# Quantised feed-forward: single-precision rows turned by TensorE, input rows weighted by GpSimd in two passes

## The reference

```
def activation_quant(x):
    scale = 127.0 / max(max(abs(x), axis=-1), 1e-5)
    return clip(round(x * scale), -128, 127) / scale
def weight_quant(w):
    scale = 1.0 / max(mean(abs(w)), 1e-5)
    return clip(round(w * scale), -1, 1) / scale
def bitlinear(x, w, g):
    return einsum('bsd,od->bso', activation_quant(rmsnorm(x, g)), weight_quant(w))

x = layernorm(h)                       # mean and variance over the 192
u, v = bitlinear(x, w_in, g_in)        # 2 x 512 columns, split in two
y = u * silu(v)
h + bitlinear(y, w_out, g_out)         # back to 192 columns
```

## Time and profile before

| | us |
|---|---|
| median of 3 runs | 2757.29 |
| lowest and highest run | 2749.5, 2757.34 |
| profiled execution, span from first to last instruction | 2748.1 |
| profiled execution, time around its span | not given in the page |
| stretch of the 28 chunks, first transpose to last `ho` | 2322.7 to 2744.9 |
| mean granted TensorE clock over the span | 0.895 |

### The profile page before, as it was taken

How to read it: one execution, slowest core, us unless ns; L and a number is a source line. 1 busy time by engine, 2 the same in 40 slices (tenths; PEclk the granted TensorE clock), 3 DMA queues, 4 the chain that set the end, 5 groups by cost and what they waited for, 6 DMA issues and landing times. The chain is left out here.

```text
span 2748.1 us, 45420 instructions
## 1 busy us (share of the span) xinstructions
PE 2290.8 (83%) x14046; PEld 1660.5 (60%) x14047; DVE 1996.1 (73%) x5437; ACT 1551.7 (56%) x2693; POOL 1004.0 (37%) x1024
## 2 busy tenths in 40 slices
PE   8999999999996999999937999926778794666665
PEld 4444444444444888888827999925576684444443
DVE  5777777777763899999944444447698877899986
ACT  2444444444444788888734565536566551777776
POOL 1100100100000266566652444478787720344433
PEclk9999999999998999999958999957688886777776
DMA  2000000000002011111136777721111100000000
GB/s 57 0 18 13 0 18 13 0 9 1 0 0 90 16 53 51 51 52 52 51 111 221 257 252 258 238 77 50 46 48 43 46 9 22 21 26 21 26 26 26
DMA packets 69143, 162.81 MB, mean 59 GB/s; under 512 B 12977, under 2 KB 32342, under 8 KB 68702
## 3 DMA queue, kind: packets, MB, share of 16 engines
q1 hardware_dynamic: 39426, 94.27, 10.4%
q0 software_dynamic: 21504, 44.99, 5.8%
q10 hardware_dynamic: 8064, 21.68, 2.6%
HBM read 63.98 MB, written 63.88 MB: 47 GB/s over the span
## 5 line engine op out<-in xcount | busy, mean ns | idle before, releaser
L211 ACT ACTIVATE prob<-pscore 128x896 f32<-128x896 f32 x336 | 308.0, 917 | 423.9 <-PE pscore L293 423.9
L418 DVE TENSOR_REDUCE pmax<-ppre 112x1 f32<-112x512 f32 x656 | 424.5, 686 | 162.0 <-PE ppre L260 161.9
L307 PE MATMUL pout<-prob,xkey 128*64 128x448 f32 x1344 | 328.3, 567 | 0.4 <-ACT prob L211 0.4
L260 PE MATMUL ppre<-xh,yh 49*112 49x512 f32 x656 | 291.4, 446 | 7.8 <-DVE pmax L418 4.2
L723 POOL DMA_INDIRECT rows_in<-xr,idx x224 | 241.3, 1077 | 127.1 <-DVE idx L1249 69.5
L193 POOL CAST yh<-ynext 113x448 fp32r<-113x448 f32 x28 | 17.2, 614 | 667.5 <-DVE pmax L418 639.4
L260 PEld LDWEIGHTS ppre<-xh,yh 49*112 49x112 f32 x656 | 112.7, 172 | 239.8 <-issue 103.5
L1708 POOL DMA_INDIRECT yg<-rows_out,place x224 | 229.3, 1024 | 62.4 <-issue 62.1
L293 PE MATMUL pscore<-yh,xh 49*128 49x448 f32 x700 | 241.1, 422 | 0.4 <-DVE yh L438 0.4
L2223 POOL TENSOR_TENSOR yg<-y,gout 112x512 f32<-112x512 f32 x112 | 141.1, 1270 | 258.6 <-DVE y L2456 258.6
L1558 POOL TENSOR_TENSOR zl<-z,zh 128x448 fp32r<-128x448 f32 x126 | 144.5, 1147 | 218.3 <-ACT zh L1524 208.8
(11 more groups left out here) (388 smaller groups left out, 6558.0 us busy)
## 6 DMA issues: line engine op xcount, KB each, us to landing
wd<-down SPq DMA_DIRECT2D x63, 512.0 KB, 3.0
xb<-rows_in SPq DMA_DIRECT2D x63, 448.0 KB, 3.6
rows_out<-yb ACTq DMA_DIRECT2D x63, 336.0 KB, 3.1
out<-ho SPq DMA_DIRECT2D x28, 336.0 KB, 2.8
rows_in<-zero SPq DMA_DIRECT2D x15, 448.0 KB
rows_in<-xr,idx POOLq DMA_INDIRECT x224
yg<-rows_out,place POOLq DMA_INDIRECT x224
xkey<-in_xkey SPq DMA_DIRECT2D x4, 800.0 KB, 6.6
```

The source lines that it names most:

```text
L211: nc.scalar.activation(prob[j % 3][:, :, :], pscore[j % 2][:, :, 0:CH], ACT.Exp).then_inc(exped, 1)
L260: pe.matmul(out[:, :], yh1[rows, q * T:(q + 1) * T], xh[b % 2][rows, block * 512:(block + 1) * 512], start=True, stop=True, tile_position= ...
L307: mm = pe.matmul(pout[i * LO:(i + 1) * LO, 0:CH], xkey[b % 2][:, 2 * j + i, :], prob[j % 3][:, i, :], start=(j == 0), stop=(i == 1 and j = ...
L418: nc.vector.reduce_max(pmax[:, q, 2 * block + half:2 * block + half + 1], bank(u, depth), AX.X).then_inc(pre_max, 1)
```

## The change

Four things change together.

- `xq` and `yq`, the bf16 copies of the rounded rows, are gone, and with them VectorE's subtraction and ScalarE's `whole_y`. TensorE turns `xr` and `yr` themselves, in single precision, with the f32 identity `eye`. MAGIC is subtracted where ScalarE copies the turned rows out of PSUM (`bias=-MAGIC`, to bf16).
- `pxt` and `pyt` give way to one PSUM tile `ptr` of three banks. A group of four transposes fills 448 columns of one bank; the groups go round the three banks, numbered by `first_x` and `first_y`, and each is copied out by itself: four copies for y and two for x, in place of two and one.
- `weigh_in` moves from VectorE to GpSimd and becomes two instructions for the whole chunk, `xd` = `h` - mean and `xg` = `xd` x `gin`. It runs three chunks ahead, behind `root_of(g)`.
- `xg` has two buffers.

```diff
+            def weigh_in(g):
+                if g:
+                    pool.wait_ge(S["xg_out"], g)
+                nc.gpsimd.tensor_tensor(xd[:], h[:, g * TPC:(g + 1) * TPC, :],
+                                        mean[:, g * TPC:(g + 1) * TPC].unsqueeze(2).broadcast_to([T, TPC, D]),
+                                        ALU.subtract).then_inc(S["xd_out"], 1)
+                pool.wait_ge(S["xd_out"], g + 1)
+                if g >= 2:
+                    pool.wait_ge(S["xr_out"], g - 1)
+                nc.gpsimd.tensor_tensor(xg[g % 2][:], xd[:], gin[:].unsqueeze(1).broadcast_to([T, TPC, D]),
+                                        ALU.mult).then_inc(S["xg_out"], 1)
+
+            pool.wait_ge(S["gin_in"], 16)
+            weigh_in(0)
+            weigh_in(1)
...
             for g in range(NC):
+                if g == 0:
+                    weigh_in(2)
                 weigh(g, 0)
                 weigh(g, 1)
                 root_of(g)
+                if g + 3 < NC:
+                    weigh_in(g + 3)
...
             def transpose_y(g):
-                pe.wait_ge(S["yq_out"], 2 * g + 2)
-                for half in range(2):
-                    for k in range(2):
-                        for q in range(TPC):
-                            mm = pe.transpose(pyt[:, half, k * CH + q * T:k * CH + (q + 1) * T],
-                                              yq[:, q, (2 * half + k) * 128:(2 * half + k + 1) * 128], eyeb[0:T, 0:T])
-                    mm.then_inc(S["ytr_mm"], 1)
+                pe.wait_ge(S["ya_out"], g + 1)
+                pe.wait_ge(S["yr_out"], g + 1)
+                for k in range(4):
+                    n = first_y[g] + k
+                    if n >= 3:
+                        pe.wait_ge(S["tr_out"], n - 2)
+                    for q in range(TPC):
+                        mm = pe.transpose(ptr[:, n % 3, q * T:(q + 1) * T], yr[:, q, k * 128:(k + 1) * 128],
+                                          eye[0:T, 0:T])
+                    mm.then_inc(S["tr_mm"], 1)
...
-            def whole_y(g, pair):
-
-                act.wait_ge(S[("ya_out", "yr_out")[pair]], g + 1)
-                nc.scalar.activation(yq[:, 2 * pair:2 * pair + 2, :], yr[:, 2 * pair:2 * pair + 2, :],
-                                     ACT.Copy, bias=-MAGIC).then_inc(S["yq_out"], 1)
-
             def take_y(g):
-                for half in range(2):
-                    act.wait_ge(S["ytr_mm"], 2 * g + half + 1)
-                    nc.scalar.copy(yT[:, 2 * half:2 * half + 2, :],
-                                   pyt[:, half, 0:2 * CH].rearrange("p (k c) -> p k c", k=2)).then_inc(S["yT_out"], 1)
+                for k in range(4):
+                    n = first_y[g] + k
+                    act.wait_ge(S["tr_mm"], n + 1)
+                    nc.scalar.activation(yT[:, k, :], ptr[:, n % 3, 0:CH], ACT.Copy, bias=-MAGIC).then_inc(
+                        S["tr_out"], 1)
...
-            def weigh_in(g):
-
-                for q in range(TPC):
-                    t = g * TPC + q
-                    ins_ = nc.vector.scalar_tensor_tensor(xg[:, q, :], h[:, t, :], mean[:, t:t + 1], gin[:],
-                                                          ALU.subtract, ALU.mult)
-                ins_.then_inc(S["xg_out"], 1)
...
                 for q in range(TPC):
-                    ins_ = nc.vector.tensor_scalar(xr[:, q, :], xg[:, q, :], sx[:, q:q + 1], MAGIC, ALU.mult, ALU.add)
+                    ins_ = nc.vector.tensor_scalar(xr[:, q, :], xg[g % 2][:, q, :], sx[:, q:q + 1], MAGIC, ALU.mult, ALU.add)
                 ins_.then_inc(S["xr_out"], 1)
-                dve.wait_ge(S["xr_out"], g + 1)
-                if g:
-                    dve.wait_ge(S["xtr_mm"], g)
-                nc.vector.tensor_scalar(xq[:], xr[:], MAGIC, None, ALU.subtract).then_inc(S["xq_out"], 1)
```

More of the change, by code:

```diff
@@ L2161, in bit_ffn_phase @@
         tmp2 = sb("tmp2_5", [T, NT])
-        xg = sb("xg5", [T, TPC, D])
+        xd = sb("xd5", [T, TPC, D])
+        xg = [sb(f"xg5_{i}", [T, TPC, D]) for i in range(2)]
         xr = sb("xr5", [T, TPC, D])
-        xq = sb("xq5", [T, TPC, D], BF16)
         xT = sb("xT5", [KC, 2, CH], BF16)
@@ L2194, in bit_ffn_phase @@
         out_t = out.rearrange("b (t p) d -> p (b t) d", p=T)
+        first_x, first_y, turned = [0], [], 2
+        for g in range(NC):
+            if g:
+                first_y.append(turned)
+                turned += 4
+            if g + 1 < NC:
+                first_x.append(turned)
+                turned += 2
+        first_y.append(turned)
         @block.sync
@@ L2244, in transpose_in @@
             def transpose_in(g):
-                if g:
-                    pe.wait_ge(S["xT_out"], g)
-                pe.wait_ge(S["xq_out"], g + 1)
-                for q in range(TPC):
-                    for c in range(2):
-                        mm = pe.transpose(pxt[:, c, q * T:(q + 1) * T], xq[:, q, c * KC:(c + 1) * KC], eyeb[0:T, 0:T])
-                mm.then_inc(S["xtr_mm"], 1)
+                pe.wait_ge(S["xr_out"], g + 1)
+                for c in range(2):
+                    n = first_x[g] + c
+                    if n >= 3:
+                        pe.wait_ge(S["tr_out"], n - 2)
+                    for q in range(TPC):
+                        mm = pe.transpose(ptr[0:KC, n % 3, q * T:(q + 1) * T], xr[:, q, c * KC:(c + 1) * KC],
+                                          eye[0:T, 0:T])
+                    mm.then_inc(S["tr_mm"], 1)
             def into(g, q):
@@ L2263, in transpose_y @@
             def transpose_y(g):
-                pe.wait_ge(S["yq_out"], 2 * g + 2)
-                for half in range(2):
-                    for k in range(2):
-                        for q in range(TPC):
-                            mm = pe.transpose(pyt[:, half, k * CH + q * T:k * CH + (q + 1) * T],
-                                              yq[:, q, (2 * half + k) * 128:(2 * half + k + 1) * 128], eyeb[0:T, 0:T])
-                    mm.then_inc(S["ytr_mm"], 1)
+                pe.wait_ge(S["ya_out"], g + 1)
+                pe.wait_ge(S["yr_out"], g + 1)
+                for k in range(4):
+                    n = first_y[g] + k
+                    if n >= 3:
+                        pe.wait_ge(S["tr_out"], n - 2)
+                    for q in range(TPC):
+                        mm = pe.transpose(ptr[:, n % 3, q * T:(q + 1) * T], yr[:, q, k * 128:(k + 1) * 128],
+                                          eye[0:T, 0:T])
+                    mm.then_inc(S["tr_mm"], 1)
             def enter(g):
-                pe.wait_ge(S["xT_out"], g + 1)
+                pe.wait_ge(S["tr_out"], first_x[g] + 2)
                 into(g, 0)
@@ L2315, in take_x @@
             def take_x(g):
-                act.wait_ge(S["xtr_mm"], g + 1)
-                nc.scalar.copy(xT[:, :, :], pxt[:, :, :]).then_inc(S["xT_out"], 1)
+                for c in range(2):
+                    n = first_x[g] + c
+                    act.wait_ge(S["tr_mm"], n + 1)
+                    nc.scalar.activation(xT[:, c, :], ptr[0:KC, n % 3, 0:CH], ACT.Copy, bias=-MAGIC).then_inc(
+                        S["tr_out"], 1)
             def silu(g, q):
@@ L2378, in _ @@
         def _(dve):
-            def weigh_in(g):
-                for q in range(TPC):
-                    t = g * TPC + q
-                    ins_ = nc.vector.scalar_tensor_tensor(xg[:, q, :], h[:, t, :], mean[:, t:t + 1], gin[:],
-                                                          ALU.subtract, ALU.mult)
-                ins_.then_inc(S["xg_out"], 1)
             def largest_in(g):
                 dve.wait_ge(S["xg_out"], g + 1)
-                nc.vector.tensor_reduce(am[:], xg[:], AX.X, ALU.max, apply_absolute_value=True).then_inc(S["am_out"], 1)
+                nc.vector.tensor_reduce(am[:], xg[g % 2][:], AX.X, ALU.max, apply_absolute_value=True).then_inc(S["am_out"], 1)
             step = [0]
```

33 lines of the change are left out of this document (13 added, 20 removed).

## The result

| | before | after |
|---|---|---|
| median of the runs, us | 2753.39 (4 runs, 2749.41 to 2757.34) | 2797.32 (4 runs, 2796.96 to 2797.73) |
| ratio after to before, 95% interval | 1 | 1.0156 [1.014, 1.0171] |
| span of the profiled execution, us | 2748.1 | 2795.9 |
| mean granted TensorE clock over the span | 0.895 | 0.892 |
| mean period of the first 24 chunks, us | 14.61 | 16.79 |

The kernel became 44 us slower. The forecast was slower by 71 us, with 2768 to 2860 us as its range. Direction and mechanism hold, the size was too large. Ratios leave out two slow runs: one of e3 (4511.79 us) and one of the kernel before beside e5 to e8 (3732.81 us, granted clock 0.547).

What follows compares the result with a forecast made beforehand. The bound was taken as a chain of waits through ScalarE, TensorE and VectorE, period 14.52 us. 25 x (2.66 + 0.19) = 71 us on the 2748.1 us span, with 9.2 around it, gave 2828 us, range 2768 to 2860.

Steps and rivals of the forecast that it cites:

- The collision: Behind root `r`, VectorE's small steps stand still until GpSimd's running pass ends, delaying `yr` by 2.66 us a chunk.
- A: Rival for the small steps: no collision that matters, VectorE works as if alone; 2732 us, faster; chance 12%.
- B: Rival for the small steps: only pass one stands in the way, +1.1 us a chunk; 2789 us; chance 13%.
- D: Rival for GpSimd's passes: each takes 2.54 us, stall +4.1 us a chunk; 2864 us; chance 10%.
- C: Rival for TensorE: collision, but its clock stays high, tile 2's products lose 0.8 us; 2808 us; chance 10%.
- The stall of +2.66 us: Small steps behind `r`: `yr` starts at P + 4.51 against P + 1.85, in each of 25 chunks.
- `s2` to the third `y`, +0.19 us: TensorE's stretch: dropping `yq` saves 1.90 us, slower f32 transposes cost 2.09; 7.80 us against 7.61.
- The idle stretch: TensorE's idle time before the transposes: 4.05 us before, nearly 5 us after, so the low clock was assumed.
- the other end: High-clock bound for `s2` to the third `y`: 5.5 us, -2.1 us a chunk.
- Start of the stage, taken as 0: GpSimd's first two passes run while VectorE waits for the weights, the third collides a little: 0 us.
- The last three chunks: Chunks 25 to 27 have no passes and no stall; periods of 14 to 15 us.
- the forecast's own mechanism: Small steps stand behind both passes and f32 transposes run at the low clock: 2808 to 2848 us, chance 55%.

Runs made afterwards that it cites:

- e3: Changed kernel with GpSimd's two passes moved from behind the root to between the second and third products of a chunk: 2753.94 us, ratio 0.9997 to before.
- e5: Changed kernel with TensorE kept busy by 18 discarded products in its idle stretch before the y transposes: 2755.61 us, ratio 1.0049 to before.
- e8: Changed kernel with each GpSimd pass cut into four instructions of 112x192, same place and work: 2756.04 us, ratio 1.0037 to before.
- e2: Kernel before with only GpSimd's two passes, `xd` and two `xg` buffers added; `xq`, `yq` and bf16 transposes stay: 2802.34 us, ratio 1.0168 to before.
- e1: Changed kernel with the weighing back on VectorE, no GpSimd passes; f32 transposes, three banks and two `xg` buffers stay: 2729.09 us, ratio 0.9902 to before.
- e4: Changed kernel with one wait added, so GpSimd's passes begin only once `s2` is written: 2815.18 us, ratio 1.022 to before.

## Why the prediction was right, and where its sizes were off

- **The collision.** Right, and it is the cause. The steps named (COPY of `s`, TENSOR_SCALAR of `am`) grew, the third one slipped between the passes as forecast, and each ends 0.02 to 0.03 us behind the pass it met. e2 shows that the passes alone make the whole loss, e3 that the loss goes with their place, e8 that it goes with the length of one GpSimd instruction. Rivals A (no collision) and B (only pass one) fall with the same rows, and D (passes of 2.54 us) with their 1.47 and 1.81. C (the clock stays high) fails in most chunks: the third `y` comes 7.92 to 8.04 us behind `s2` in 16 of the first 25. In two of them it came at 6.68 and 6.69, as C has it.
- **The stall of +2.66 us.** This is the term that was mis-sized: `yr` starts at P + 3.92, P being the end of `r` (2552.90), not at P + 4.51, so +2.07. The first pass, which reads `mean` with stride 0, takes 1.47 us and not 1.82. It also starts at once, 0.03 before `r`'s end by the rows, where 0.10 behind it was assumed. The second pass took 1.81 against 1.82. It began 0.07 us behind the first, where 0.17 was assumed. The COPY was forecast at 1.4 us and took 0.75: `ho` stands ahead of it until P + 0.71 as forecast, so the length should have been read as P + 1.95 less P + 0.71, 1.24; the rest is the shorter and earlier pass. Over the 25 chunks the term is 25 x 0.59 = 15 us too large.
- **`s2` to the third `y`, +0.19 us.** It came as 7.92 to 8.04 for 7.80, so +0.3 to +0.4, in 16 chunks; in the mean of the periods e2 and after differ by 0.20. The 24 transposes took 2562.74 - 2558.21 = 4.53 us to the first product, 0.19 each, where 24 x 0.179 = 4.30 was forecast. The mean of 16.79 lies below the typical 17.03 because in some chunks the clock rose early: in the two with periods of 15.67 and 15.68 the sixteen still took 3.23 and 3.24 us, but the eight of x 0.96 and 0.97 in place of 1.70, and the products of tile 2 ran fast too. The idle stretch was forecast at nearly 5 us and was 4.17, the smaller stall again.
- **The f32 transposes cost time only at the low clock.** The prediction took that level as given behind the stall, which was right in most chunks, and named the other end: the third `y` 5.5 us behind `s2`. In four of e1's first 25 chunks it came at 5.50 to 5.52, in e5 without overrun at 5.38. In the mean e1 gained 0.69 us a chunk. Of 2.87 us a chunk that the passes cost in the f32 kernel, 2.07 are the standstill; the other 0.8 is what is left, and fast transposes forfeited would explain it. e5 supports the split from the other side: standstill kept, clock mended, most of the loss gone.
- **Start of the stage, taken as 0.** Wrong: the way to the first `yr` grew by 3.83 us. GpSimd's first passes fall on VectorE's last steps on `root` and `fac`, five operations with one or two inputs, all in SBUF. VectorE's timeline of the changed kernel:

```profile
2299.03 1.03 DVE L497 TENSOR_TENSOR tmp<-root 112x112 f32<-112x112 f32 x1
2300.09 1.85 DVE L498 TENSOR_TENSOR tmp<-tmp,tmp 112x112 f32<-112x112 f32 x1
2301.97 1.46 DVE L499 TENSOR_SCALAR tmp<-tmp 112x112 f32<-112x112 f32 x1
2303.46 1.90 DVE L500 TENSOR_TENSOR fac<-root,tmp 112x112 f32<-112x112 f32 x1
2305.40 1.58 DVE L2426 TENSOR_TENSOR fac<-fac,rstd 112x112 f32<-112x112 f32 x1
```

  They took 0.27, 0.27, 0.22, 0.28 and 0.28 us before: 7.82 for 1.32. Part of it is hidden, since VectorE waited 2.20 us for a DMA (`gout`) a little later in the kernel before, and its own first `xg` is gone: the first chunk's `r` ends 2.53 us later, counted from the start of the stage. The other 1.30 is that chunk's own standstill behind `r`, 3.92 us to `yr` for 2.62, which the forecast had among its 25. The prediction had the first two passes run "while VectorE still waits for the weights"; VectorE was at work there.
- **The last three chunks.** "No passes and no stall" was right, but they were priced as before. They ran 3.41 us faster in all, which fits the f32 part without its counterpart, as in e1.
- **Size.** Forecast 2.85 x 25 = 71 us. Found 52.49 + 3.83 - 3.41 - 0.69 = 52.2 us in the last stage, 19 less: 24 x 0.59 = 14.2 from the standstill, 4.1 from the end, 1.7 from the rest of the period, less 1.0 more than forecast at the start. The ratio, 1.0156, is 43 us at 2753.39; forecast 2828, measured 2797. That is in the stated range, but below the 2808 to 2848 that was given to the forecast's own mechanism, which is the one that was found. Rival B gave 2789, nearer by the number, but its mechanism isn't there.

## What to carry to other kernels

Work moved to GpSimd is not free because GpSimd has a hole: first look at what VectorE does in that hole, and how tiny and serial it is, since there a small COPY, TENSOR_SCALAR or TENSOR_TENSOR out of SBUF can grow to the length of a GpSimd instruction. In this kernel the weighing was best left on VectorE (e1). If the work must run there, cut it into short instructions, or put it where VectorE isn't on the path, and check what GpSimd then delays. When two edits come together, time each alone: here one was worth 1%, and the other, which cost 1.7%, also took away what the first one gave.

## What the runs showed of the hardware

- A TENSOR_TENSOR with both inputs in SBUF stands as well as a COPY or a TENSOR_SCALAR: 1.85 us in place of 0.27 at the start of the stage, and `am` 0.42 in place of 0.16 in e8. The prediction had left that open. A RECIPROCAL of 112x4 did not stand: in e8's first chunk it began 0.11 us into a quarter of `xd` and took its 0.18 us, while the COPY, TENSOR_TENSOR and TENSOR_SCALAR ahead of it took 0.45, 0.42 and 0.43. That is one event: in the other chunks of the stage it fell outside or at the edge of the passes.
- Where a VectorE instruction is waiting when a GpSimd instruction ends, it gets its turn and does not wait for the next GpSimd instruction as well (after, e4 and e8). In e8 GpSimd then stands in turn: quarters of `xg` last 0.77 us in place of 0.59 where VectorE's `yr` came between. So the standstill is set by the length of one GpSimd instruction, not by that of the series.
- A GpSimd TENSOR_TENSOR of 112x768 takes 1.81 us with `gin` repeated over the tiles, and 1.47 us with one number repeated over each row (`mean`, stride 0). At 112x192 it is 0.59 undisturbed and 0.51 (e8). The one multiplies and the other subtracts, so no run shows that the stride alone makes the difference.
- Sixteen f32 transposes of 112x128 took 3.25 us at 0.50 and 1.79 at 1.00 (e5). Sixteen in bf16 took 1.68 at 0.50. f32 ones at the high level are as fast as bf16 ones at the low.
- TensorE's clock depends on what the engine did before, and not on the last idle stretch alone. Behind 4.17 us the sixteen transposes ran at 0.50 in the changed kernel, behind 2.09 us (e1) part of them ran fast; but behind 1.15 us in another chunk of e1 they took 3.25 us again, and there the products ahead had run slow as well (pairs in 1.06 us, for 0.59 at the high level). Why some chunks have a partly high clock (periods of 15.67 to 16.4 among those of 17.0 in the changed kernel) and others not was not settled.
